# Second attention: sums and reciprocal of a group of four heads issued ahead of the second half of its values

## The reference, cut to what matters

```
k = apply_rope(k, cos, sin)
attn = jnp.einsum('bhnd,bhsd->bhns', q, k) * scale
attn = jnp.clip(attn, -11.0, 11.0)
attn = jax.nn.softmax(attn, axis=-1)
out = jnp.einsum('bhns,bhsd->bhnd', attn, v)
out = out.transpose(0, 2, 1, 3).reshape(b, n, INNER)
return out @ Wo + bo
```

## Time and profile before

| what | value |
|---|---|
| median of 3 runs | 284.77 us (283.45 to 284.98) |
| the profiled execution: time | 283.72 us |
| the profiled execution: span from first to last instruction | 282.0 us |
| PE busy in the span | 245.0 us (87%) |
| DVE busy | 175.9 us (62%) |
| ACT busy | 117.0 us (42%) |
| POOL busy | 45.1 us (16%) |
| stretch of the second attention's passes 1 to 6, by PE's rows | 191.5 to 252.7 us |

### The profile page before, as it was taken

How to read it: one execution, slowest core, us unless ns; L and a number is a source line. 1 busy time by engine, 2 the same in 40 slices (tenths; PEclk the granted TensorE clock), 3 DMA queues, 4 the chain that set the end, 5 groups by cost and what they waited for, 6 DMA issues and landing times.

```text
span 282.0 us, 5073 instructions
## 1 busy us (share of the span) xinstructions
PE 245.0 (87%) x2004; PEld 157.2 (56%) x2004; DVE 175.9 (62%) x387; ACT 117.0 (42%) x180; POOL 45.1 (16%) x65
## 2 busy tenths in 40 slices
PE   0642969999999989999999999999979999999952
PEld 0232323333334547888888677886646668666550
DVE  0671038998885441465656963067986975799544
ACT  0226314466667875243434334454434432444000
POOL 2419100000000100052331643001200000110010
PEclk9995579999999999999999999999999999999995
DMA  6958446238722200005106062510000000000001
GB/s 127 236 152 118 104 127 127 74 96 301 206 85 69 75 3 0 2 0 122 31 1 149 2 143 53 132 46 3 0 2 2 0 2 2 0 2 3 0 3 38
DMA packets 13517, 18.63 MB, mean 66 GB/s; under 512 B 2204, under 2 KB 8212, under 8 KB 13204
## 3 DMA queue, kind: packets, MB, share of 16 engines
q1 hardware_dynamic: 9246, 11.95, 18.3%
q10 hardware_dynamic: 4246, 6.34, 8.0%
HBM read 12.45 MB, written 1.45 MB: 49 GB/s over the span
## 4 chain that ended last, share of the span: by engine, by line
PE 67%; DVE 13%; DMA 11%; issue 3%; ACT 2%; POOL 1%; SPq 1%; DVEq 0%; ACTq 0%; POOLq 0%
PE b L857 41%; PE st L857 24%; DMA reg_q<-q_scr 5%; DVE nmax L663 4%; DMA x<-in_x 2%; DVE reg_p L796 2%; DVE rs L808 2%; DMA m_scr<-mpart 2%; DMA q_scr<-reg_z 2%; ACT reg_p L582 1%; PE b L956 1%; ACT reg_p L541 1%; POOL rstd L405 1%; PE b L861 1%; SPq L348 0%
## 5 line engine op out<-in xcount | busy, mean ns | idle before, releaser
L663 DVE TENSOR_REDUCE nmax<-b 128x1 f32<-128x512 f32 x64 | 41.3, 685 | 21.7 <-PE b L857 21.4
L857 PE MATMUL b<-reg_p,v 128*32 128x256 f32 (+1 forms) x768 | 50.3, 382 | 1.3 <-ACT reg_z L547 1.1
L582 ACT ACTIVATE reg_p<-st 128x1024 f32<-128x1024 f32 x32 | 31.0, 1022 | 44.4 <-PE st L857 44.4
L559 ACT ACTIVATE reg_z<-st,b 128x256 f32<-128x256 f32 x56 | 24.5, 473 | 32.8 <-PE st L857 32.8
L541 ACT ACTIVATE reg_p<-st 128x1024 f32<-128x1024 f32 x32 | 31.9, 1022 | 9.6 <-PE st L857 6.7
L857 PEld LDWEIGHTS b<-w,reg_z 128*128 128x128 f32 x256 | 30.8, 192 | 4.9 <-issue 4.5
L857 PEld LDWEIGHTS b<-reg_p,v 128*32 128x32 f32 (+1 forms) x768 | 19.9, 102 | 22.3 <-issue 9.8
L857 PE MATMUL st<-v,reg_k 64*128 64x256 f32 x256 | 32.0, 389 | 0.3 <-ACT reg_p L582 0.2
L857 PE MATMUL b<-w,reg_z 128*128 128x128 f32 x256 | 31.5, 276 | 0.0
L796 DVE TENSOR_SCALAR reg_p<-reg_p 128x1024 f32<-128x1024 f32 x32 | 22.5, 703 | 11.2 <-ACT reg_p L582 11.1
L857 PEld LDWEIGHTS st<-v,reg_k 64*128 64x128 f32 x256 | 23.7, 186 | 7.9 <-issue 3.8
(11 more groups left out here) (158 smaller groups left out, 265.5 us busy)
## 6 DMA issues: line engine op xcount, KB each, us to landing
reg_k<-k_scr SPq DMA_DIRECT2D x6, 384.0 KB
w<-in_w ACTq DMA_DIRECT2D x1, 2048.0 KB, 9.3
reg_k<-reg_p SPq DMA_DIRECT2D x16, 128.0 KB, 2.3
reg_k<-reg_q SPq DMA_DIRECT2D x16, 128.0 KB, 2.3
reg_q<-q_scr SPq DMA_DIRECT2D x6, 192.0 KB
k_scr<-reg_z SPq DMA_DIRECT2D x6, 128.0 KB
ctxT<-in_ctxT SPq DMA_DIRECT2D x2, 256.0 KB, 8.8
reg_p<-in_wv ACTq DMA_DIRECT2D x1, 512.0 KB, 10.0
```

The source lines that it names most:

```text
L559: nc.scalar.activation(hT[:, n % 2, f, :], hidden(n, f), ACT.Relu, bias=b1[:, n % E, f:f + 1]).then_inc(h_sb, 1)
L582: nc.scalar.activation(prob[:, u % RING1, :], st2[u % 2][:, :], ACT.Exp, scale=DK1 ** -0.5).then_inc(st_exp, 1)
L663: nc.vector.tensor_reduce(nmax[:, q, i:i + 1], bank[4 + mx % 2], AX.X, ALU.max, negate=True).then_inc(mx_done, 1)
L857: return nc.tensor.matmul(o, l, r, start=start, stop=stop)
```

## The change

In the loop over the passes, for passes 1 to 6, the sums and the reciprocal of group g-1 are placed ahead of the second half of the values of that group. Pass 7 and the group behind it are as they were. Nothing is added or removed.

```
             order.append(("s1", 2 * g + 1))
             if g == 2:
                 order.append(("l1t", 1))
-            order += [("o1", g - 1, 1), ("os", g - 1), ("rec", g - 1), ("nrm", g - 1)]
+            order += [("os", g - 1), ("rec", g - 1), ("o1", g - 1, 1), ("nrm", g - 1)]
             if g == G + 1:
                 order.append(("lnf", 0))
```

## The result

The changed kernel takes 285.38 us in the median of 16 executions (283.27 to 287.67), the kernel before 283.22 us in the median of 16 (280.09 to 285.52). The ratio is 1.0086, with a 95% interval of 1.0050 to 1.0121: slower by 2.2 us by the medians, 2.4 us by the ratio. The profiled execution took 285.48 us, with a span of 283.7 us (282.0 before). Both kernels scatter by about 4 us, so single times say little. What follows leans on a stretch inside the traces that leaves most of that scatter out: from the first queries of pass 1 to the scores of pass 3. Before it is 210.71 - 191.52 = 19.19 us.

The account below looks back on a forecast made before the run. The prediction took PE to set the pace through passes 1 to 5, with DVE on the chain from 240.62 to 262.53 us. It added 0 + 0 + 0.8 us to a median of 284.77 us: 285.6 us, range 283.9 to 286.9.

Parts of the forecast that it names:

- The new wait in pass 2: Behind the transposition, PE's sums wait for ACT's L564 to empty bank 7: a new pause, taken as 0.8 us.
- The exchange as such: Values and sums trading places on PE in six passes: taken as 0, with bounds of 0 to 0.7 us.
- Rival B: Each exchange costs up to 0.12 us in all six passes, 0.7 us more: 286.3 us, chance 0.10.
- The bound of 0.12 us at sums to values: Upper bound for PE's step from sums to values, not shown alone in the trace; the lower bound was 0.
- The earlier reciprocal: Sums end 1.75 us earlier; DVE's reciprocal gains at most 0.65 us, in pass 2 alone, not reaching the end: 0.
- Nothing absorbs it: Behind pass 2, PE's back-to-back work and DVE's part of the chain from 240.62 us both move by 0.8 us.
- Rivals C and D: C: the pause in pass 2 is hidden, 284.8 us, chance 0.13. D: the earlier reciprocal pays, 284.1 us, chance 0.07.
- The sum: Exchange 0, reciprocal 0 and new wait in pass 2 0.8 us: +0.8 us, median 285.6 us (+0.28%), chance 0.62.
- rival A: PE's clock falls in the new pause of pass 2, costing 1.7 us more: 287.3 us, slower by 0.9%, chance 0.08.
- the signs of being wrong: No pause in pass 2, a second wait in pass 1 or 5, sums and values above 2.75 us, shorter DVE chain.

Follow-up runs that it names:

- run 1: The kernel before with the exchange of sums and values made in pass 2 only: median 285.23 us, ratio 1.0004 to the kernel before.
- run 5: The changed kernel itself, measured again over six executions: median 286.38 us, ratio 1.0118 to the kernel before.
- run 6: The changed kernel with both pauses of PE in pass 2 filled by unused extra products: median 284.74 us, ratio 1.0044 to the kernel before.
- run 10: The changed kernel with only its first pause in pass 2 filled by unused extra products: median 284.28 us, ratio 0.9985 to the kernel before.
- run 2: The kernel before with the exchange made in passes 1 and 3 to 6, not in pass 2: median 283.34 us, ratio 1.0003 to the kernel before.
- run 8: The changed kernel with the norm and transposition of pass 2 made earlier: median 283.19 us, ratio 0.9962 to the kernel before.
- run 9: The changed kernel itself, measured a third time: median 285.57 us, ratio 1.0103 to the kernel before.
- run 3: The changed kernel with only the second pause of pass 2, at the sums, filled by unused products: median 285.07 us, ratio 1.0019 to the kernel before.
- run 12: The kernel before with the norm for the transposition made later, its pause 3.12 us, no exchange: median 287.24 us, ratio 1.0126 to the kernel before.
- Run 7: The kernel before with its 1.69 us pause ahead of the transposition filled by unused products: median 283.92 us, ratio 0.9982 to the kernel before.
- run 11: An unchanged copy of the kernel before under its own label: median 283.64 us, ratio 0.9965 to the kernel before.

## Why the prediction was partly right

*The new wait in pass 2: right.* It was forecast as 0.77 to 0.81 us at the sums, released by L564, and is 0.74 us as PE's idle time and 0.79 to 0.82 us in the stretch of the traces without a fall (runs 1, 5, 6, 10). It was the only one; passes 1, 3, 4, 5 and 6 show none.

*The exchange as such: right.* 2.73 us for the pair in both orders; run 2 shows no cost in time, run 8 none in the stretch. Rival B falls. The bound of 0.12 us at sums to values was not needed: 220.49 - 219.60 = 0.89 us is less than the 0.98 us that sums take ahead of scores.

*The earlier reciprocal: right.* It gains nothing anywhere, DVE's stream being the same. In pass 2 it was said to start without idle time; in the trace after it waits 0.37 us, and its product 1.08 us for the values, because both ran at half clock. In the traces without a fall (runs 5 and 10) neither waits.

*Nothing absorbs it: right up to 274 us.* The pieces of the chain on DVE behind 240 us are all late by the same 2.11 to 2.12 us. The 0.3 us that come back behind them are due to the clock at the last products, which the prediction didn't look at. Rivals C and D fall.

*The sum: wrong in one step.* "+0.8 us" took the clock to stay at 1.00, so it had the cost of a fall at nothing, and gave that case, rival A, a chance of 0.08. Rival A is what the profile after shows, at its price: 0.8 + 1.7 = 2.5 us were worked out for it, and the stretch grew by 2.50 us. The clock fell about 0.3 us behind the pause, though, and not in it. Of the signs of being wrong that the prediction named, one came: sums and values took 4.41 us, more than 2.75 us. In the four traces of the exchange in pass 2 with both pauses left in (changed kernel, runs 1, 5, 9) the clock fell in two. The medians of the changed kernel lie 2.16, 2.76 and 1.19 us above before in its three comparisons, 2.0 us in the mean; with 0.8 us of pause and 1.7 us for a fall, about 7 executions in 10 would have to have one, a rough estimate, as the intervals of the three ratios are 2 to 3 us wide. The forecast that the change would read as none was wrong: slower by 0.86% was measured, and 0.15 had been given for slower by over 0.5%. That the forecast of 285.6 us and the measured 285.38 us agree is luck: the sum began from 284.77 us, the median of before over three executions, and that median is 283.22 us over 16. Two errors of opposite sign, 1.55 us at the start and 1.4 us at the change, cancel.

What argued against A was that a pause of 1.69 us "did nothing", and that the transposition breaks the new one. The first was one trace, and the second didn't keep the clock up. The row that spoke for A, the fall at a pause of 2.72 us, was the better guide, since the new wait makes one stretch of 1.70 + 0.41 + 0.74 us with little in it out of that pause. The Trainium skill's warning in "TensorE: Matmul & The Clock Gate", section "A second HAM failure mode: psum-queue depth-cycling", that short pauses between groups of matmuls can cost clock, was cited and set aside on the same ground. The trace after agrees with it as far as one fall and one return behind two short pauses go, with 0.55 over 3.8 us of unbroken work; it shows no swinging back and forth.

*What brings the clock down.* Five traces have the exchange in pass 2 and the first pause left in (changed kernel, runs 1, 3, 5, 9), and three of them have a fall. The two with the first pause filled (runs 6 and 10) have none, and their medians lie 1.64 us (run 6 below run 5) and 1.29 us (run 10 below run 9) lower on the same chip. Filling only the second pause doesn't prevent a fall (run 3), and lengthening the first to 3.12 us without any exchange gives one (run 12). This points to the first pause as the one that matters, with the exchange adding to it. It isn't shown beyond doubt, since the same program falls in one execution and holds in another, and two traces without a fall can be chance. Run 7 adds nothing here, as before has no fall with its pause either.

Not settled: before, with the same first pause, has no fall in three traces (before, runs 2, 11), yet run 3 had one behind hardly more. Whether before falls in some of its executions can't be told from times that scatter by 4 us. What decides between fall and hold in one program, and how often each comes, stays open; it would take more traces.

## What to carry to other kernels

A wait that is moved out of its cover can cost more than its length if TensorE has just been waiting: here 2.50 us for a pause of 0.8 us in two of four traces. Add up the pauses around the place, and price the half clock that may follow from a row of the same kernel. Putting an instruction with a wait directly behind the one whose output must first be read out of the same bank exposes that read; work that waits for nothing in between, here 1.75 us of values, hides it. Where one pause of the bound engine is known, take it away before anything is moved around it: here the norm made earlier gave 1.55 us in the stretch, and with it in place the exchange is free in the stretch. The early norm without the exchange has the lowest median of the versions that ran (281.74 us, 0.9957); the two can't be told apart in the stretch, 17.64 us for both.

## What the runs showed of the hardware

The clock fell in the middle of almost unbroken work, 1.5 us after a pause had ended (run 3), and the same program fell in one execution and held in the next (changed kernel, runs 5 and 9). It stayed at half for 3.4 us in pass 2 of the changed kernel and of runs 3 and 9, and for 6.8 us in run 12, of which 5.9 us were work.

A part of the scatter of 4 us goes with the clock much earlier in the execution. The queries of pass 1 start at 188.79 us in run 9, 191.52 us before and 193.03 us in run 1, with a mean clock from 20 to 60 us of 0.87, 0.79 and 0.74. The clock isn't all of it: at a mean of 0.79 these queries start anywhere from 190.34 us (run 3) to 193.60 us (run 5), and which of the two causes the other isn't shown.

```profile
20.00:60.00 40.00, 29.12 (x93) 12.06 (x94) 23.18 (x43) 18.00 (x30) 9.25 (x12) 0.87 0.52 113
```

```profile
20.00:60.00 40.00, 29.45 (x72) 11.97 (x72) 18.66 (x31) 14.40 (x27) 9.23 (x12) 0.74 0.50 101
```

The first is run 9, the second run 1. Execution 9 took 281.4 us of span with a fall in pass 2 in it, less than the 282.0 us of before without one: a single time of this kernel can't show a change of 2 us.
